# Last phase of a decoder block: attention rows and their norms moved into the first MLP, head norms in token blocks, transposes released earlier

## The chip, the cores and the metric

The kernel runs on one core of one Trainium2 chip. A core has TensorE (PE in the profile, its weight loads PEld), VectorE (DVE), ScalarE (ACT), GpSimd (POOL), and SyncE (SP), which here only issues DMAs. The metric is the device time of one execution, in microseconds: 1348.08 is the median of three runs (1347.18 to 1348.21).

## The reference

Eight sequences of 512 tokens with 256 features pass through a layer norm and causal attention (16 heads), then cross attention to a short context followed by an MLP, then a second MLP with ternary weights. In short:

```
x1  = x  + attention(layernorm(x)) @ Wout + bout
Q   = layernorm(x1)                           # the residual base of the cross block
q   = layernorm(Q)*g1+b1 @ wq                 # 16 heads of 64
qn  = q / max(||q||_head, 1e-12)
x'  = Q + (qn . N) + bo                       # N = keys, values and wo folded per sequence
x2  = x1 + x' + gelu(layernorm(x')*g2+b2 @ w1 + b1) @ w2 + b2
out = x2 + gelu(layernorm(x2) @ W1t + b1) @ W2t + b2
```

Since cross attention has no softmax, the context side is folded into one matrix N per sequence before this phase.

## The kernel before

The program has four phases, one after the other: projections, attention, preparation of N and the ternary weights, and `mix_phase` (L1392 to L2126), in which everything after attention is computed. Only the last one is changed, besides a table of constants (`head_selectors`, L82). It fills the trace from about 625 us to the end.

All weights and features are in two parts, a rounded high part and a low part (`fh`/`fl`, `bh`/`bl`, `hh`/`hl`), and a product is three matmuls. A round of `mix_phase` works on two sequences at once: the front of one (attention rows, query tiles, cross attention) and the back of the one before it (both MLPs). There are nine rounds: one with a front only, seven with both (six of them load more work, the seventh loads none), and one with a back only. Below they are rounds 0 to 8.

A round is a list of units in a fixed order: `order(back, front)` (L1417) gives 8 query tiles Q, 8 tiles M of the first MLP, 8 cross tiles X, and 8 tiles T of the ternary MLP. PE *begins* a unit (`begin`, which fills one of three PSUM tiles `psG`) and *finishes* it three units later (`finish`, `rows_of`: 12 matmuls of 256 columns that add to row sums in `psY`). In between, ACT and DVE (for X also POOL) make the high and low parts of the unit. Each engine's program is written out by hand in that same order, and each works through its own queue in order. T is a stage of its own: Q, M and X run on into one another, T starts and ends with an empty pipeline.

`psY` is two pairs of banks. Pair 0 holds the rows of M, then of X; pair 1 holds the norms' head sums, then the attention rows, then the rows of T. A pair must be read by DVE before PE opens it again (`pair_free`, `open_rows` L1966).

Normalised rows `z` are transposed by PE into the single PSUM tile `psT`, one half of the features at a time: `z_first` waits for `z`, `z_second` waits until the low part of the first half is made (`z_parts`), `z_split` does so for the second half. This happens three times a round:

- z1, the query norm of the *next* sequence: attention rows on PE after the last M unit, `add_attention` on DVE in X unit 5, `moments` in X unit 7, `rsqrt_twice` on POOL, `z1` in T unit 2, transposes after T units 4 and 6 (`Z1_AT`). In round 0 `z1` and its transposes stand after X, so that round 1 begins behind them.
- z2, for M: made by DVE at the head of a round, transposed after Q units 3 and 5 (`Z2_AT`). In round 8 it stands alone before M.
- z3, for T: from `add_mlp` and its moments on DVE in X unit 2, transposed after X units 4 and 6.

The head norms of q: ACT squares the query tiles, `head_sums` adds them over heads on PE into a 128x512 tile (32 rows for each of four query tiles, all 512 tokens), ACT takes the root after M unit 3 (`NORMS_AT`), DVE inverts and splits (`inverse_norms`, L1773 to L1780), all over 512 columns:

```
stepped(nc.vector.tensor_scalar(n2[:, :], n2[:, :], 1e-12, None, ALU.max))
stepped(nc.vector.reciprocal(n2[:, :], n2[:, :]))
stepped(nc.vector.tensor_copy(rh[:, :], n2[:, :]))
```

POOL adds biases at the head of a round (`biased`, three operations over 128x1024), and adds `base` later, once DVE has read the old one (`base_free`). DVE's `prepare_o` makes the high and low parts of the next attention output, also at the head of a round.

## Time and profile before

| | us |
|---|---|
| median of three runs | 1348.08 |
| the profiled execution | 1350.23 |
| its span, first to last instruction | 1348.4 |
| PE busy over the span | 1046.7 (78%) |
| DVE / ACT / POOL busy | 788.7 / 663.5 / 425.9 |
| one middle round, query tile to query tile | 79.86 |
| PE busy in it | 72.04 |

The page gives busy time for the whole program, and the last phase is about half of it. For this change the timeline of PE in one round is the view to read: whatever stops PE there is listed behind its rows in brackets, as the idle time before the instruction and the line it waited at (L1966 opens a pair, L1986 `z_first`, L1991 `z_second`, L1996 `z_split`, L2023, L2035 and L2045 wait for the parts of an M, X and T unit, L2060 for the inverse norms). The median stands 2.15 us below the profiled execution.

### The profile page before, as it was taken

What the parts mean: (1) busy time and instruction counts of PE and PEld (TensorE: products, weight loads), DVE (VectorE), ACT (ScalarE), POOL (GpSimd) and SP (SyncE); (2) the same over time, 40 slices, a digit from 0 to 9 for tenths busy, and PEclk for the clock granted to TensorE, in tenths of its full rate; (3) what the DMA queues carried; (4) which work ended last, traced back from release to release, by engine and by line L of the source; (5) the groups of instructions that cost most, each with busy time, mean ns of one, the idle gap of its engine ahead of it and who ended that gap; (6) DMA issues with size and microseconds to landing.
All of it is one profiled execution on the core that took longest, in us unless ns stands there. A gap on an engine that the chain in (4) does not pass through costs nothing. (4 is left out here: it accounts for less than half of the span.)

```text
span 1348.4 us, 22433 instructions
## 1 busy us (share of the span) xinstructions
PE 1046.7 (78%) x6749; PEld 751.9 (56%) x6749; DVE 788.7 (58%) x1680; ACT 663.5 (49%) x1166; POOL 425.9 (32%) x556
## 2 busy tenths in 40 slices
PE   3777058788999985783566989899898999988875
PEld 2444023343444433672454877778687786867764
DVE  3888356576777743863444655746656574655523
ACT  1334115565666673461225466473655747465433
POOL 0344226566333331110422231524313242330301
PEclk9677558999999996896777999999999999999987
DMA  2332423333222103257202040301203030020000
GB/s 85 103 116 74 124 92 111 114 120 105 90 96 93 58 31 135 117 223 287 57 26 84 1 125 0 109 16 44 81 0 116 8 108 16 0 78 1 10 7 16
DMA packets 52716, 103.72 MB, mean 77 GB/s; under 512 B 6640, under 2 KB 32496, under 8 KB 48560
## 3 DMA queue, kind: packets, MB, share of 16 engines
q1 hardware_dynamic: 49484, 95.53, 21.0%
q0 software_dynamic: 1920, 6.03, 1.4%
q10 hardware_dynamic: 1252, 1.39, 0.3%
q8 instruction: 33, 0.54, 0.2%
q14 instruction: 27, 0.22, 0.1%
HBM read 62.96 MB, written 39.58 MB: 76 GB/s over the span
## 5 line engine op out<-in xcount | busy, mean ns | idle before, releaser
L804 ACT ACTIVATE p_probs<-p_psS 128x512 f32<-128x512 f32 (+1 forms) x352 | 180.8, 563 | 122.3 <-ACTq L803 120.0
L706 DVE CUSTOM_DVE_ANT_0 p_psA<-p_psA,p_mask 128x512 f32<-128x512 f32 (+1 forms) x256 | 155.5, 647 | 103.9 <-DVEq L704 103.6
L1771 DVE TENSOR_TENSOR p_hl<-p_h,p_hh 128x512 fp32r<-128x512 f32 x128 | 86.9, 688 | 153.1 <-DVEq L1770 151.1
L838 PE MATMUL p_psA<-p_ks,p_qs 96*128 96x512 bf16 (+3 forms) x512 | 144.1, 317 | 37.0 <-PEq L836 36.7
L857 PE MATMUL p_psS<-p_qs,p_ks 99*128 99x256 bf16 (+3 forms) x512 | 131.1, 310 | 20.0 <-PEq L882 11.4
L1656 ACT ACTIVATE p_h<-p_psG,w_columns 128x512 f32<-128x512 f32 x128 | 88.3, 690 | 94.4 <-ACTq L1655 94.0
L725 POOL TENSOR_SCALAR_AFFINE_SELECT p_probs<-p_probs 128x512 f32<-128x512 f32 x128 | 80.8, 635 | 130.8 <-POOLq L724 113.8
L1975 PE MATMUL p_psY<-p_n,p_hh 128*128 128x256 f32 x512 | 105.3, 289 | 12.5 <-PEq L2035 7.6
L868 PE MATMUL p_psO<-p_probs,p_v 128*32 128x512 f32 (+3 forms) x1024 | 92.8, 457 | 26.6 <-PEq L864 25.2
L857 PEld LDWEIGHTS p_psS<-p_qs,p_ks 99*128 99x128 bf16 x512 | 44.0, 98 | 106.8 <-issue 91.8
L1697 ACT ACTIVATE p_hh<-p_h 128x512 fp32r<-128x512 f32 x64 | 40.4, 632 | 118.8 <-ACTq L1696 118.8
L1975 PEld LDWEIGHTS p_psY<-p_n,p_hh 128*128 128x128 f32 x512 | 84.4, 192 | 18.9 <-issue 18.1
L1616 POOL TENSOR_TENSOR p_base<-p_x,p_q0b 128x1024 f32<-128x1024 f32 x8 | 19.2, 2405 | 223.2 <-POOLq L1615 223.2
L1657 ACT ACTIVATE p_hh<-p_psG,w_columns 128x512 fp32r<-128x512 f32 x128 | 87.8, 686 | 0.0
L838 PEld LDWEIGHTS p_psA<-p_ks,p_qs 96*128 96x128 bf16 x512 | 51.6, 101 | 59.5 <-issue 47.4
L1975 PE MATMUL p_psY<-w_w_hi,p_hh 128*128 128x256 f32 x256 | 72.4, 283 | 11.1 <-PEq L2023 11.1
L1981 PE MATMUL p_psT<-p_ident,p_z 128*128 128x128 f32 x192 | 32.7, 298 | 57.8 <-PEq L1986 31.6
L1975 PE MATMUL p_psY<-p_n,p_hl 128*128 128x256 f32 x256 | 72.8, 284 | 0.0
L1975 PE MATMUL p_psY<-w_t,p_hh 128*128 128x256 f32 x256 | 65.3, 291 | 8.8 <-PEq L1966 4.7
L1975 PE MATMUL p_psY<-w_w_hi,p_hl 128*128 128x256 f32 x256 | 71.5, 279 | 0.0
L1975 PE MATMUL p_psY<-w_w_lo,p_hh 128*128 128x256 f32 x256 | 71.3, 279 | 0.0
L710 DVE TENSOR_REDUCE p_mx<-p_psA 128x2 f32<-128x512 f32 (+1 forms) x96 | 66.3, 693 | 3.8 <-DVEq L704 0.6
(244 smaller groups left out, 2811.6 us busy)
## 6 DMA issues: line engine op xcount, KB each, us to landing
p_n<-n_parts SPq DMA_DIRECT2D x16, 1024.0 KB, 6.8
o_sums<-p_o SPq DMA_DIRECT2D x32, 256.0 KB, 2.9
n_parts<-p_nh SPq DMA_DIRECT2D x8, 1024.0 KB, 3.9
n_parts<-p_nl SPq DMA_DIRECT2D x8, 1024.0 KB, 6.0
q_parts<-p_part SPq DMA_DIRECT2D x48, 128.0 KB
p_qs<-q_parts SPq DMA_DIRECT2D x32, 192.0 KB
p_x<-in_x_dram SPq DMA_DIRECT2D x8, 512.0 KB, 4.2
p_qs<-q_parts SPq DMA_DIRECT2D x32, 128.0 KB
```

The lines of the kernel that those rows point to most:

```text
L706: nc.vector.tensor_tensor_reduce(out=bank[:, 0:w], in0=bank[:, 0:w], in1=mask[:, S - w:S], scale=1.0, scalar=MASKED, op0=ALU.add, op1=ALU.max,
L710: nc.vector.tensor_reduce(mx[:, h:h + n, i], bank[:, 0:n * w].rearrange("p (r k) -> p r k", r=n), AX_X, ALU.max).then_inc(A_free, 1)
L725: nc.gpsimd.affine_select(square, square, [[0, G], [1, P]], ALU.is_ge, 0.0, base=0, channel_multiplier=-1).then_inc(masked, 1)
L804: nc.scalar.activation(probs[:, g % 2, at:at + n * w], psS[place(s, turn) % SB][:, 0:n * w], ACT.Exp, scale=SCALE).then_inc(exp_done, 1)
L838: last = nc.tensor.matmul(bank[:, z * w:(z + 1) * w], qs[0:SROWS, k, g * G + r0 + z, i * P:(i + 1) * P], ks[0:SROWS, k, g, 0:w], start=Tru ...
L857: last = nc.tensor.matmul(bank[:, z * w:(z + 1) * w], key, qs[0:SROWS + MROWS, k, h, j * P:S], start=True, stop=True)
L868: last = nc.tensor.matmul(psO[32 * r:32 * r + 32, j * P:S], v[:, k, g, j, :], probs[:, g % 2, at:at + w], start=(j == 0), stop=(j == TT - 1))
L1656: nc.scalar.activation(h[:, u % LAG, :], psG[u % LAG][:, :], ACT.Gelu, bias=bias[:, m:m + 1])
L1657: nc.scalar.activation(hh[:, u % LAG, :], psG[u % LAG][:, :], ACT.Gelu, bias=bias[:, m:m + 1]).then_inc(h_ready, 1)
L1697: nc.scalar.activation(hh[:, s, :], h[:, s, :], ACT.Copy).then_inc(qh_dve if m < POOL_FROM else qh_pool, 1)
L1771: nc.vector.tensor_tensor(hl[:, s, :], h[:, s, :], hh[:, s, :].bitcast(F32), ALU.subtract).then_inc(h_parts, 1)
L1975: last = nc.tensor.matmul(dst, xx[:, toks], ww[:, k, :], start=(k == 0 and t % 2 == 0 and i == 0), stop=(last_k and t % 2 == 1 and i == le ...
```

## The change

Four things are done.

1. **Attention rows and z1 move forward.** In rounds with a back, PE's attention rows come after M unit 2 (`ROWS_AT`) instead of after M unit 7; DVE's `add_attention`, `moments` and `z1` come at M units 3, 4 and 6; POOL's `rsqrt_twice` stands before z3's; the transposes of z1 come after M unit 6 and X unit 0, and ACT reads them after X units 0 and 2. In round 0 the attention rows stand before X and z1 within X. In round 7, z2 of the last round is made and transposed within T.
2. **Norms by token blocks.** The four groups of 32 rows now hold the four blocks of 128 tokens, and all 16 heads (high and low copy) within each. The root, the maximum, the reciprocal and the rounding work on 128x128; four small operations write the low/high signs into a block-diagonal `rs` (128x512, cleared once). `head_sums` is 16 matmuls of 128 columns instead of 4 of 512. ACT takes the root after M unit 1.
3. **`psT` is free once read.** A new semaphore `T_free` is raised by ACT behind a drain after it has read the tile twice (`affine`), or by DVE after `plain_low`; `z_first` and `z_second` wait for it, and `z_split` for both low parts.
4. **`base`** is made in `q0b` at the head of the round, without waiting for the old one.

```diff
-        Z1_AT = (4, 6)
-        NORMS_AT = 3
+        Z1_AT, Z1_READ = (M, 6, X, 0), (0, 2)
+        Z1_FIRST, Z1_FIRST_READ = (3, 5), (5, 7)
+        NORMS_AT, ROWS_AT, ADD_AT, MOMENTS_AT, Z1_MADE = 1, 2, 3, 4, 6
...
-        n2 = sb("n2", [P, S], F32)
-        rh, rs = sb("rh", [P, S], F32R), sb("rs", [P, S], F32R)
+        n2 = sb("n2", [P, P], F32)
+        rh, rs = sb("rh", [P, P], F32R), sb("rs", [P, S], F32R)
...
                     biased(q0b, q0, B2).then_inc(pool_step, 1)
+                    pool.wait_ge(pool_step, 1)
+                    pool.sem_inc(pool_step, -1)
+                    nc.gpsimd.tensor_tensor(q0b[:, :, :], x1[:, :, :], q0b[:, :, :], ALU.add).then_inc(base_ready, 1)
                     if more:
                         rows_in()
-                    pool.wait_ge(pool_step, 1)
-                    pool.sem_inc(pool_step, -1)
-                    if back:
-                        pool.wait_ge(base_free, 1)
-                        pool.sem_inc(base_free, -1)
-                    nc.gpsimd.tensor_tensor(base[:, :, :], x1[:, :, :], q0b[:, :, :], ALU.add).then_inc(base_ready, 1)
+                if more:
+                    rsqrt_twice()
...
                 nc.scalar.activation(hi[:, c, :], psT[:, :], ACT.Identity, bias=b[:, c:c + 1], scale=g[:, c:c + 1]).then_inc(z_done, 1)
+                act.drain().then_inc(T_free, 1)
...
                         nc.scalar.activation(hh[:, s, :], h[:, s, :], ACT.Copy).then_inc(qh_dve if m < POOL_FROM else qh_pool, 1)
+                        read = Z1_READ if back else Z1_FIRST_READ
+                        if more and m in read:
+                            affine(fh, w["ln1_g"], w["ln1_b"], read.index(m))
...
-                nc.vector.scalar_tensor_tensor(out=rs[:, :], in0=rh[:, :].bitcast(F32), scalar=minus, in1=n2[:, :],
-                                               op0=ALU.mult, op1=ALU.add).then_inc(rn_ready, 1)
+                for b in range(TB):
+                    rows = slice(32 * b, 32 * b + 32)
+                    last = nc.vector.scalar_tensor_tensor(out=rs[rows, b * P:(b + 1) * P], in0=rh[rows, :].bitcast(F32),
+                                                          scalar=minus[rows, :], in1=n2[rows, :], op0=ALU.mult, op1=ALU.add)
+                last.then_inc(rn_ready, 1)
...
                         if not back and m == XT - 1:
                             inverse_norms()
+                            add_attention(False)
+                            stepped(moments(x1))
+                            aggregate(mv1, var1_ready)
...
             def z_second():
-                pe.wait_ge(z_parts, 1)
-                pe.sem_inc(z_parts, -1)
+                pe.wait_ge(T_free, 1)
+                pe.sem_inc(T_free, -1)
                 transpose_rows(1)
...
-                for r in range(4):
-                    last = nc.tensor.matmul(sums[32 * r:32 * r + 32, :], select[:, j, :], sq[:, (4 * j + r) % SQ, :],
-                                            start=(j == 0), stop=(j == 1))
+                for t in range(4 * j, 4 * j + 4):
+                    for b in range(TB):
+                        last = nc.tensor.matmul(sums[32 * b:32 * b + 32, 0:P], select[:, t, :], sq[:, t % SQ, b * P:(b + 1) * P],
+                                                start=(t == 0), stop=(t == XT - 1))
...
-                            if kind == M and m == XT - 1 and front and more:
+                            if more and back and kind == M and m == ROWS_AT:
                                 attention_rows()
...
+                            if more and back and (kind, m) == Z1_AT[:2]:
+                                z_first()
+                            if more and back and (kind, m) == Z1_AT[2:]:
+                                z_second()
```

What the change does to the order shows on DVE first. In the names, `p_hl` is the low part of a unit, `p_n` the norms, `p_x<-p_psY,p_xin` is `add_attention`, `p_x<-p_psY,p_base` is `add_mlp`, `p_h<-p_psG,p_q` scales a cross tile. This is DVE in a middle round, from the end of `prepare_o` through the M units, before:

```order
L1733 TENSOR_TENSOR p_ol<-p_o,p_oh 128x1024
L1771 TENSOR_TENSOR p_hl<-p_h,p_hh 128x512 x5
L1776 TENSOR_SCALAR p_n<-p_n 128x512
L1777 RECIPROCAL p_n<-p_n 128x512
L1778 CAST p_rh<-p_n 128x512
L1779 SCALAR_TENSOR_TENSOR p_rs<-p_rh,p_select,p_n 128x512
L1771 TENSOR_TENSOR p_hl<-p_h,p_hh 128x512 x3
```

and after:

```order
L1734 TENSOR_TENSOR p_ol<-p_o,p_oh 128x1024
L1773 TENSOR_TENSOR p_hl<-p_h,p_hh 128x512 x2
L1778 ISA
L1779 TENSOR_SCALAR p_n<-p_n 128x128
L1780 RECIPROCAL p_n<-p_n 128x128
L1781 CAST p_rh<-p_n 128x128
L1784 SCALAR_TENSOR_TENSOR p_rs<-p_rh,p_signs,p_n 32x128 x4
L1773 TENSOR_TENSOR p_hl<-p_h,p_hh 128x512 x2
L1739 TENSOR_TENSOR p_x<-p_psY,p_xin 128x512 x2
L1823 ISA
L1824 ISA
```

The inverse norms have moved from behind the fifth low part to behind the second, and `add_attention` now stands behind the fourth, in front of the fifth to eighth.

Next, still DVE in a middle round, the end of M and the start of X (`p_stats<-p_x` are moments, of `x2` when they follow `add_mlp`), before:

```order
L1785 TENSOR_TENSOR p_h<-p_psG,p_q 128x512 x2
L1790 TENSOR_TENSOR p_hl<-p_h,p_hh 128x512 x2
L1738 TENSOR_TENSOR p_x<-p_psY,p_base 128x512 x2
L1799 ISA
L1875 ISA
L1744 BN_STATS p_stats<-p_x 128x6 x4
L1785 TENSOR_TENSOR p_h<-p_psG,p_q 128x512
L1749 BN_AGGR p_mv<-p_stats 128x2 x4
L1790 TENSOR_TENSOR p_hl<-p_h,p_hh 128x512
```

and after:

```order
L1745 BN_STATS p_stats<-p_x 128x6 x4
L1750 BN_AGGR p_mv<-p_stats 128x2 x4
L1773 TENSOR_TENSOR p_hl<-p_h,p_hh 128x512 x2
L1755 TENSOR_SCALAR p_z<-p_x,p_mv,p_both 128x256 x4
L1773 TENSOR_TENSOR p_hl<-p_h,p_hh 128x512
L1791 TENSOR_TENSOR p_h<-p_psG,p_q 128x512 x2
L1796 TENSOR_TENSOR p_hl<-p_h,p_hh 128x512 x2
L1739 TENSOR_TENSOR p_x<-p_psY,p_base 128x512 x2
L1805 ISA
L1745 BN_STATS p_stats<-p_x 128x6 x4
L1791 TENSOR_TENSOR p_h<-p_psG,p_q 128x512
L1750 BN_AGGR p_mv<-p_stats 128x2 x4
```

The moments of the attention rows and `z1` now stand between the low parts of M units 4 to 7, so the last low part and the first scaled cross tile come behind `z1`.

Last, ACT in a middle round from the last M unit through X (`p_hh<-p_h` is the high part of a cross tile, `p_bh<-p_psT` a read of z3), before:

```order
L1656 ACTIVATE p_h<-p_psG,w_columns 128x512
L1657 ACTIVATE p_hh<-p_psG,w_columns 128x512
L1697 ACTIVATE p_hh<-p_h 128x512 x7
L1673 ACTIVATE p_bh<-p_psT 128x512
L1697 ACTIVATE p_hh<-p_h 128x512
L1673 ACTIVATE p_bh<-p_psT 128x512
```

and after:

```order
L1659 ACTIVATE p_hh<-p_psG,w_columns 128x512
L1697 ACTIVATE p_hh<-p_h 128x512
L1669 ACTIVATE p_feat<-p_psT,w_columns 128x512
L1670 ACTIVATE p_fh<-p_psT,w_columns 128x512
L1697 ACTIVATE p_hh<-p_h 128x512 x2
L1669 ACTIVATE p_feat<-p_psT,w_columns 128x512
L1670 ACTIVATE p_fh<-p_psT,w_columns 128x512
L1697 ACTIVATE p_hh<-p_h 128x512 x4
L1676 ACTIVATE p_bh<-p_psT 128x512
```

The two pairs of reads of z1 stand now behind the first and the third cross tile; before they stood among the T units.

## Rows read from the trace of the kernel before

**Rows 1.** Busy time by stretch: length, then busy us (instructions) per engine, clock, DMA.
```profile
660.93:721.50 60.57, 37.23 (x200) 30.19 (x201) 30.21 (x51) 18.46 (x30) 22.16 (x18) 0.78 0.18 61
...
801.75:881.61 79.86, 72.04 (x458) 60.79 (x457) 47.74 (x90) 45.70 (x71) 25.48 (x21) 1.00 0.16 53
...
1201.01:1287.55 86.54, 70.05 (x434) 58.60 (x433) 43.56 (x79) 43.52 (x69) 19.32 (x13) 0.97 0.04 13
```

**Rows 2.** Timeline, PE, one middle round: start us, us, line, instruction, idle before it.
```profile
812.43 0.63 PE L1981 MATMUL p_psT<-p_ident,p_z 128*128 128x128 f32 x4 [1.64 <-PEq L1991]
...
822.29 0.33 PE L1975 MATMUL p_psY<-w_w_hi,p_hh 128*128 128x256 f32 x1
...
838.08 0.35 PE L1975 MATMUL p_psY<-w_w_hi,p_hh 128*128 128x256 f32 x1 [1.58 <-PEq L2023]
...
842.86 0.28 PE L1975 MATMUL p_psY<-w_wout_hi,p_oh 128*128 128x256 f32 x1
...
852.07 0.36 PE L1975 MATMUL p_psY<-p_n,p_hh 128*128 128x256 f32 x1 [1.00 <-PEq L2035]
...
861.41 0.47 PE L1960 MATMUL p_psG<-p_bh,w_t 128*128 128x512 f32 x1 [0.28 <-PEq L1996]
...
880.59 0.36 PE L1975 MATMUL p_psY<-w_t,p_hh 128*128 128x256 f32 x1 [0.51 <-PEq L2045]
```

**Rows 3.** Timeline, PE, the last round that has a query stage.
```profile
1244.78 0.35 PE L1975 MATMUL p_psY<-p_n,p_hh 128*128 128x256 f32 x1 [2.32 <-PEq L1966]
...
1260.45 0.47 PE L1960 MATMUL p_psG<-p_bh,w_t 128*128 128x512 f32 x1 [0.15 <-PEq L1996]
...
1276.26 0.36 PE L1975 MATMUL p_psY<-w_t,p_hh 128*128 128x256 f32 x1 [0.51 <-PEq L2045]
```

**Rows 4.** Timeline, PE, the first round, and the two joins at either end.
```profile
685.27 1.62 PE L2063 MATMUL p_psG<-p_rs,w_spread_sel 128*128 128x512 f32 x3 [7.97 <-PEq L2060]
...
689.12 0.55 PE L1975 MATMUL p_psY<-p_n,p_hh 128*128 128x256 f32 x1 [2.23 <-PEq L1966]
...
714.21 1.08 PE L1981 MATMUL p_psT<-p_ident,p_z 128*128 128x128 f32 x4 [6.16 <-PEq L1986]
...
721.50 0.76 PE L1960 MATMUL p_psG<-p_fh,w_wq_hi 128*128 128x512 f32 x1 [2.56 <-PEq L1996]
...
742.43 0.33 PE L1975 MATMUL p_psY<-w_w_hi,p_hh 128*128 128x256 f32 x1
...
1280.72 0.63 PE L1981 MATMUL p_psT<-p_ident,p_z 128*128 128x128 f32 x4 [3.29 <-PEq L1986]
...
1287.55 0.77 PE L1960 MATMUL p_psG<-p_bh,w_w_hi 128*128 128x512 f32 x1 [2.56 <-PEq L1996]
```

**Rows 5.** Lines by form, L868 in the attention phase: count, busy us, mean ns.
```profile
L868 PE MATMUL p_psO<-p_probs,p_v 128*32 128x512 f32 x184 | 24.6, 602 | 11.4 <-PEq L864 11.4
...
L868 PE MATMUL p_psO<-p_probs,p_v 128*32 128x128 f32 x176 | 8.9, 273 | 0.0
```

**Rows 6.** Timeline, DVE: the first round's end, and the same middle round.
```profile
708.20 1.29 DVE L1738 TENSOR_TENSOR p_q<-p_psY,p_q 128x512 f32<-128x512 f32 x2 [2.52 <-DVEq L1823]
...
810.26 2.02 DVE L1761 TENSOR_TENSOR p_bl<-p_feat,p_bh 128x512 fp32r<-128x512 f32 x1 [3.65 <-DVEq L1760]
...
815.39 1.22 DVE L1731 TENSOR_TENSOR p_o<-p_o,p_ol 128x1024 f32<-128x1024 f32 x1
...
832.51 3.35 DVE L1777 RECIPROCAL p_n<-p_n 128x512 f32<-128x512 f32 x1
```

**Rows 7.** Timeline, POOL, the same middle round.
```profile
811.70 2.83 POOL L1589 TENSOR_TENSOR p_xin<-p_xin,p_biases 128x1024 f32<-128x1024 f32 x1
...
861.48 0.20 POOL L1566 TENSOR_TENSOR p_var<-p_mv,p_eps 128x4 f32<-128x4 f32 x1
...
865.85 0.20 POOL L1586 TENSOR_TENSOR p_both<-p_var,p_rstd 128x4 f32<-128x4 f32 x1 [0.18 <-POOLq L1568]
```

**Rows 8.** Timeline, ACT, just before the same middle round.
```profile
796.61 0.78 ACT L1667 ACTIVATE p_feat<-p_psT,w_columns 128x512 f32<-128x512 f32 x1 [0.47 <-ACTq L1666]
```

More of the change, by code:

```diff
@@ L1676, in round_ @@
                 units = order(back, front)
-                if back and not front:
-                    for c in range(C):
-                        affine(bh, w["ln2_g"], w["ln2_b"], c)
                 for u, (kind, m) in enumerate(units):
@@ L1704, in round_ @@
                         gelu(w["fb1"], u, m)
-                        if more and m in Z1_AT:
-                            affine(fh, w["ln1_g"], w["ln1_b"], Z1_AT.index(m))
-                if more and not back:
-                    for c in range(C):
-                        affine(fh, w["ln1_g"], w["ln1_b"], c)
+                        if front and not more and m == XT - 1:
+                            for c in range(C):
+                                affine(fh, w["ln2_g"], w["ln2_b"], c)
             act.wait_ge(act_go, 1)
@@ L1925, in round_ @@
                             aggregate(mv2, var2_ready)
-                        if more and m == 5:
-                            affine_low(fl, fh, 0)
-                        if more and m == 7:
-                            affine_low(fl, fh, 1)
+                        if front and not more and m == 5:
+                            z2()
+                        if front and not more and m == 7:
+                            for c in range(C):
+                                affine_low(fl, fh, c)
             nc.vector.memset(eps[:, :], EPS)
+            nc.vector.memset(rs[:, :].bitcast(F32), 0.0)
             stepped(nc.vector.memset(mhalf[:, :], -0.5))
@@ L2070, in round_ @@
                 stages = [units[:-XT], units[-XT:]]
-                if back and not front:
-                    z_first()
-                    z_second()
-                    z_split()
                 at = 0
@@ L2105, in round_ @@
                                 z_second()
-                            if kind == T and more and m == Z1_AT[0]:
+                            if front and not more and kind == T and m == 7:
                                 z_first()
-                            if kind == T and more and m == Z1_AT[1]:
-                                z_second()
                     at += len(stage)
-                if more and not back:
-                    z_first()
-                    z_second()
+                if not back:
+                    z_split()
             for i in range(2):
                 pe.sem_inc(pair_free[i], 1)
+            pe.sem_inc(T_free, 1)
             pe.wait_ge(consts, 1)
```

129 lines of the change are left out of this document (73 added, 56 removed).

## The prediction

> **What bounds the kernel now.** I read the busy time by stretch first, then PE's timeline of one middle round, and then, wherever PE stands idle in it, the other engines at that moment.
>
> A middle round takes 79.86 us, of which PE is busy 72.04 at a clock of 1.00 [rows 1]. DVE has 47.7, ACT 45.7 and POOL 25.5. So PE is the bound of these rounds, and what can be won is the idle time between its instructions. The first stretch of the phase is different: of 60.57 us PE is busy 37.23, at a mean clock of 0.78. The reader is to see that the ends of the phase are far looser than its middle.
>
> In a middle round PE is idle at [rows 2]: the second transposes of z2 (1.64, it waits for a low part), the last M units (1.58, DVE is in the inverse norms), an X unit (1.00), the start of T (0.28) and its last units (0.51). The rest lies in T, where z1 is transposed. At the ends: 7.97 for the inverse norms of round 0; transposes at 714.21 and query tiles at 721.50 behind X in round 0; and 3.29 and 2.56 before M of round 8 [rows 4].
>
> **Middle rounds, 1 to 6.** I cut the round at four places where PE's timeline has a row before, and build the same stretch for after. Units from the same timeline: a tile of six matmuls 1.41 us, 12 rows matmuls 1.40, 24 of them (attention rows) 2.80, a spread of X 0.24, four transposes 0.36 plus 0.2 when PE had been idle. These are spacings of the rows around those in [rows 2].
>
> *Query to the first M rows* (801.75 to 822.29, 20.54 us). `z_second` no longer waits for DVE, only for ACT's two reads: PE is there at 810.6, ACT is done at about 810.3. That gives back 1.64 and the restart, 2.0. Two things are lost. POOL now runs four operations of 2.4 us in a row at the head of the round, not three. DVE's low part at 810.26 shows what this means: 2.02 us where it needs 0.69, because it starts only when POOL's operation ends at 811.70; and the POOL operation that begins there takes 2.83, longer by DVE's part [rows 6, 7]. They alternate. So the second low part is done at about 815.2 and M begins 0.4 late; `prepare_o`, which starts at 815.39 now, starts at 817.5 and ends at 820.9; M's first low part comes behind it at 821.5, where PE asks at 820.6: 1.0 lost. Sum: 20.54 - 2.0 + 0.4 + 1.0, less 0.1 for restarts: 19.85.
> The Trainium skill has this twice. Advanced Engine Details and Errata, section "Mode Summary", says that GpSimd and DVE block each other when DVE is in a two-port mode; by that alone a low part, a sum of two tensors, would not be held, and the round would keep the 1.4 us. GPSIMD Engine Reference, section "Key points", adds DVE operations with two inputs in SBUF. The row at 810.26 is such an operation and was held, so the sum goes by it.
>
> *M rows to the end of M* (822.29 to 842.86, 20.57 us). The wait of 1.58 goes. The reciprocal takes 3.35 us over 512 columns [rows 6], so about 0.85 over 128; the whole of `inverse_norms` falls from 5.4 to about 2.4, and comes where PE does not ask for it. Added: attention rows 2.8 and the first transposes of z1, 0.55. The path of z1 just fits: attention rows end at 831.5, add 1.5, a low part 0.6, moments 1.4 and their aggregation 0.5, POOL's chain 4.6 (861.48 to 866.05, [rows 7]), z1 1.4, together 10.2; PE has 7 x 1.41 + 0.24 = 10.1 of units in between. Sum: 20.57 - 1.8 + 2.8 + 0.55 = 22.1.
>
> *X* (842.86 to 861.41, 18.55 us with 2.8 of attention rows in it). Those rows stood on PE while DVE added the MLP's sums, which X's rows wait for (they share a pair of banks). Without them the wait is open. Round 7 loads no attention rows and shows the price: 2.32 us at 1244.78 [rows 3]. The change adds to it. ACT now reads z1 between the first and the second cross tile, two operations of 0.67 (the row at 796.61 has 0.78 with its tail, [rows 8]) and a drain, and DVE's `add_mlp` stands behind the low part of that second tile: 1.7 more, so 4.0. The second transposes cost 0.5, and the two low parts of z1 on DVE, 0.6 each, come before the third and fourth unit of the chain DVE, ACT, POOL, so the wait of 1.00 at 852.07 grows to 1.6. Sum: 18.55 - 2.8 + 4.0 + 0.5 + 0.6, less 0.6 of small idle behind that wait: 20.2.
>
> *T* (861.41 to 881.61, 20.20 us). z1 leaves it. Round 7's T has no z1: from its start to its last wait it takes 1276.26 - 1260.45 = 15.81, a middle round 880.59 - 861.41 = 19.18 [rows 2, 3]. That is 3.37 less: 16.85.
>
> The round comes to 19.85 + 22.1 + 20.2 + 16.85 = 79.0, a gain of 0.9 of a round. The four stretches change by -0.7, +1.5, +1.7 and -3.4. Round 1 counts from its first M rows, so five and three quarters of these: -5.
>
> **Head sums.** They become 64 records of 128 columns in place of 16 of 512 in each round. Kept concurrent over the four column groups, the columns are the same and the cost is 0. The attention phase has both shapes: 184 records of 512 in 24.6 us and 176 of 128 in 8.9 [rows 5], 0.134 and 0.051 each. By these 32 records take 1.6 us where 8 take 1.07, the most it can cost: 0.55 for each group, 16 groups, 9 us. I take 0, as the 8.9 us hold the tail behind each group, and keep 9 as a bound.
>
> **Round 0 and its join to round 1.** Before X, 7.97 of idle [rows 4] shrinks by the shorter inverse norms (3.0) and root (0.35), but attention rows (2.8) fill that time and DVE adds them (3.4 with moments) before it scales the first cross tile. X's rows start at 688.3 instead of 689.12: -0.8. Attention rows leave X: -2.8. X ends at 704.5, where it now ends about 708.0 (DVE's next operation is at 708.20, [rows 6]). From there PE now has to wait for moments, z1, and twice for transposes, ACT and DVE, until 721.50 [rows 4]: 13.5 us. All of this lies within X after the change, and the queries of round 1 begin at 704.6: -16.9. Two covers go with it. z2 still needs X's result: add 1.5, `base` 1.3, moments and aggregation 1.9, POOL 1.5, z2 1.4, so it is ready at 712.3, and PE asks at 710.2: 2.1. And POOL's four operations start 4.3 us later against PE than in a middle round, so M's first low part comes 3.2 late, 2.2 more than above. Against these stands the slow start of the query tiles (0.76 at 721.50, 1.5 in all). Sum at the first M rows of round 1 (now 742.43): -16.9 + 2.1 + 2.2 - 1.5 = about -14.
>
> **Round 7, round 8.** Round 7 gains 1.6 in Q (no `prepare_o` behind the low parts) and 1.6 in M: -3.2. z2 of round 8 is made within T of round 7. PE is done there at 1277.4 and begins M at 1287.55 [rows 3, 4]. After, the second transposes wait for ACT's reads of the first (0.9 and 0.55 of their own), the last rows end at 1278.45, ACT reads until 1278.95, DVE's low part ends at 1279.65, M begins at 1279.8: -7.7. And M begins at the high clock: the first tile at 1287.55 shows 0.77 for a matmul that takes 0.47 at 861.41 [rows 2, 4], about 1.9 over four microseconds. Sum -12.8.
>
> The prologue has one wait shortened by DVE's low part (0.7) and two copies of constants more or larger on SP's queue. I take 0, with a microsecond either way.
>
> **Sum.** -5 -14 -12.8 = -31.8: the profiled execution of 1350.2 becomes 1318.4, its span 1316.6. The median of the runs is 2.15 below the profiled one, so the runs come to 1316.3.
>
> **The rivals.**
> *A, the clock falls in X.* PE idles 4.0 us before X's rows in each middle round. In the trace it idled 3.29 us before 1280.72 and ran the next transposes at 2.4 GHz (0.63 for four), but 6.16 us before 714.21 and ran at 1.2 GHz (1.08) [rows 4]. Four microseconds lie between. If it falls, the rows from 689.12 (0.55 each at the start) show what follows: about 2.5 us lost before the clock is back, some hidden by the wait of 1.6. Also here: `T_free` comes as late as the low part did, 1.8 a round. Either gives 1316.3 + 6 x 2 = 1328.
> The Trainium skill (TensorE: Matmul & The Clock Gate, section "Part 1: The HAM clock gate") says that the slow state is the default and that idleness brings it back, which speaks for this rival; the trace agrees at 714.21, and not yet at 1280.72.
> *B, the middle rounds gain more.* POOL's fourth operation does not hold up `prepare_o`, and ACT's reads slip in behind the second tile: then 1.4 and 1.7 a round go. 1316.3 - 6 x 2.5 = 1301. For it: DVE in a middle round is busy 47.7 of 79.86. Against: both engines work in order, and the order is written.
> *C, slower.* The place is the start of X in the middle rounds. There z1's chain, the last low part of M, two scaled tiles, their low parts, `add_mlp`, moments and the third tile all stand in one queue on DVE, and POOL's chain of seven small operations in front of it can hold DVE up, as at 810.26. If each wait in it is longer by as much as the one there (1.3 us) at four places and the clock falls (2.5), a round costs 7.7 more than I say: 1316.3 + 46 = 1362. It decides from 5.3 a round, where it eats 31.8. For it: PE has no spare work there after the change. Against: DVE's operations that read PSUM show no such stretch while POOL works.
> *D, the head sums cost their upper bound*: 1316.3 + 9 = 1325. And the change does not do what it says if z1 is not ready at M unit 6 and PE stands there: this is inside C.
>
> **How the numbers follow.** My forecast (the middle rounds between -2.3 and +1 each) 0.58, A 0.15, D 0.04, B 0.15, C 0.08. The forecast's own range is 1308 to 1326. With A, D and half of B it is 1303 to 1334. Differences of under 0.2% (2.7 us) cannot be told from none. Only C is slower, with 0.07 of its 0.08; 0.02 lie within 0.2%; faster 0.91.
>
> **What would show it.** In the profile after: a middle round near 79.0; PE idle 3.5 to 4.5 us before the first cross rows and a clock of 1.00 behind it; idle about 1 us before the first M rows; `z_second` of z2 without a wait; T's 8 units in 16.8; a reciprocal of 0.9; query tiles of round 1 directly behind X of round 0; and M of round 8 some 2.4 us behind T of round 7. Wrong it would be with a middle round over 84, or with the clock below 0.95 in one.

## The result and the profile after

The changed kernel takes 1339.67 us (median of seven runs, 1334.74 to 1341.04) where the kernel before takes 1348.65 on the same chip. The ratio is 0.9908 (95% interval 0.9886 to 0.9929): 9 us are gained where 32 were forecast, and the time lies outside the range. The profiled execution took 1340.68, its span 1338.7.

The page of the changed kernel, its span and clock line:

```profile
span 1338.7 us, 23286 instructions
...
PEclk9677558899999996897689899898999989999997
```

The reader is to see the 8s and 7s in the second half of the clock line, one dip in each round. Before, that part was nines. The same in the windows view (stretch; us; busy us of PE, PEld, DVE, ACT, POOL; then PE's clock): round 2 in its four stretches, then all of it, then from the query tiles of round 7 to M of round 8. They answer to [rows 1].

```profile
793.82:813.66 19.84, 19.14 (x141) 14.45 (x139) 13.53 (x17) 16.83 (x27) 10.25 (x4) 1.00 0.08 26
813.66:836.64 22.98, 22.46 (x157) 20.88 (x157) 12.93 (x31) 10.59 (x17) 3.28 (x7) 1.00 0.25 68
836.64:858.80 22.16, 17.54 (x117) 16.46 (x115) 13.37 (x27) 7.93 (x13) 9.54 (x8) 0.85 0.00 0
858.80:875.69 16.89, 15.74 (x96) 13.59 (x97) 9.40 (x20) 9.90 (x16) 1.84 (x3) 1.00 0.32 124
793.82:875.69 81.87, 74.88 (x506) 65.37 (x505) 49.23 (x93) 45.25 (x71) 24.91 (x21) 0.96 0.15 51
1203.10:1279.49 76.39, 69.46 (x482) 59.86 (x481) 42.15 (x81) 43.16 (x69) 18.85 (x13) 1.00 0.02 8
```

A middle round takes 81.87 us, 2.0 more than before, with the clock at 0.85 in its third stretch. PE's timeline, first the join of rounds 0 and 1, then the waits of round 2, then rounds 7 and 8; the rows before are [rows 2 to 4]:

```profile
641.64 0.55 PE L1995 MATMUL p_psY<-w_wout_hi,p_oh 128*128 128x256 f32 x1 [23.14 <-PEq L1986]
...
662.43 0.76 PE L1980 MATMUL p_psG<-p_fh,w_wq_hi 128*128 128x512 f32 x1 [2.56 <-PEq L2018]
...
690.38 0.55 PE L1995 MATMUL p_psY<-p_n,p_hh 128*128 128x256 f32 x1 [5.21 <-PEq L1986]
...
707.33 0.39 PE L1980 MATMUL p_psG<-p_fh,w_wq_hi 128*128 128x512 f32 x1
...
715.62 0.63 PE L2001 MATMUL p_psT<-p_ident,p_z 128*128 128x128 f32 x4 [2.46 <-PEq L2008]
...
725.50 0.47 PE L1980 MATMUL p_psG<-p_bh,w_w_hi 128*128 128x512 f32 x1 [0.48 <-PEq L2018]
...
731.82 0.35 PE L1995 MATMUL p_psY<-w_w_hi,p_hh 128*128 128x256 f32 x1 [0.69 <-PEq L1986]
...
813.66 0.36 PE L1995 MATMUL p_psY<-w_w_hi,p_hh 128*128 128x256 f32 x1 [0.67 <-PEq L1986]
...
834.51 0.63 PE L2001 MATMUL p_psT<-p_ident,p_z 128*128 128x128 f32 x4 [0.52 <-PEq L2008]
...
840.68 0.55 PE L1995 MATMUL p_psY<-p_n,p_hh 128*128 128x256 f32 x1 [3.65 <-PEq L1986]
...
843.38 1.05 PE L2001 MATMUL p_psT<-p_ident,p_z 128*128 128x128 f32 x4
...
851.43 0.36 PE L1995 MATMUL p_psY<-p_n,p_hh 128*128 128x256 f32 x1 [0.81 <-PEq L2058]
...
858.80 0.48 PE L1980 MATMUL p_psG<-p_bh,w_t 128*128 128x512 f32 x1 [0.17 <-PEq L2018]
...
1243.97 0.36 PE L1995 MATMUL p_psY<-p_n,p_hh 128*128 128x256 f32 x1 [2.65 <-PEq L1986]
...
1279.49 0.47 PE L1980 MATMUL p_psG<-p_fh,w_w_hi 128*128 128x512 f32 x1 [1.60 <-PEq L2018]
```

Query tiles of round 1 begin at 707.33 directly behind X, and M of round 8 follows the last rows of T after 1.60 idle; both ends work as they were meant to. In round 2 PE waits 3.65 before X's rows (840.68) and the first matmul there takes 0.55, where the one of round 7, after a wait of 2.65 (1243.97), takes 0.36: the clock is at 1.2 GHz in the one and at 2.4 in the other. Slow rows run until 846.

Cut where the forecast cut, in the profiled executions:

| stretch | forecast | measured |
|---|---|---|
| start of the last phase to the queries of round 0 | 0 | +1.5 |
| those to the first M rows of round 1 | -14 | -12.1 |
| those to the queries of round 7 | -5 | +12.7 |
| those to M of round 8 | -10.9 | -10.2 |
| M of round 8 to the end | -1.9 | -1.6 |
| sum | -31.8 | -9.7 |

The +1.5 is not the change's: the last burst of matmuls of the phase ahead of it begins 1.7 later in this trace (615.40 against 613.67). This start moves from kernel to kernel: in the profiles of this case the queries of round 0 begin anywhere from 656.8 to 665.1. Of the 22 us that are missing, 17.7 lie in the middle rounds. Those are what the experiments are about.

### The profile page after: what moved, and what is told of

Read it like the earlier page. It is cut to its first block and busy times, and to the rows that moved or that the text cites. A ratio compares the mean times of both kernels' runs of the same rounds, so it can differ in the third digit from the quotient of the medians.

```text
span 1338.7 us, 23286 instructions
## 1 busy us (share of the span) xinstructions
PE 1062.5 (79%) x7133; PEld 781.2 (58%) x7133; DVE 798.1 (60%) x1705; ACT 660.4 (49%) x1166; POOL 423.2 (32%) x556
## 5 line engine op out<-in xcount | busy, mean ns | idle before, releaser
L1995 PE MATMUL p_psY<-p_n,p_hh 128*128 128x256 f32 x512 | 117.2, 313 | 35.8 <-PEq L1986 29.7
L1995 PEld LDWEIGHTS p_psY<-p_n,p_hh 128*128 128x128 f32 x512 | 95.6, 218 | 41.8 <-issue 41.3
L1571 POOL TENSOR_TENSOR p_var<-p_mv,p_eps 128x4 f32<-128x4 f32 x24 | 8.1, 338 | 334.0 <-POOLq L1577 201.8
L1995 PE MATMUL p_psY<-p_n,p_hl 128*128 128x256 f32 x256 | 78.9, 308 | 0.0
L1604 POOL TENSOR_TENSOR p_hl<-p_h,p_hh 128x512 fp32r<-128x512 f32 x40 | 51.3, 1295 | 46.0 <-POOLq L1603 35.1
```

Of the source, the lines that this page charges most:

```text
L1604: nc.gpsimd.tensor_tensor(hl[:, s, :], h[:, s, :], hh[:, s, :].bitcast(F32), ALU.subtract).then_inc(qn_pool, 1)
L1995: last = nc.tensor.matmul(dst, xx[:, toks], ww[:, k, :], start=(k == 0 and t % 2 == 0 and i == 0), stop=(last_k and t % 2 == 1 and i == le ...
```

## The experiments

Times are compared as ratios to the kernel before, run beside each on the same chip (1349 to 1354 us there). "A round" is the distance from the first query tile of one middle round to that of the next in the kernel's profile; rounds 2 to 6 of a kernel agree within 0.1 us, but for the run with 4 idle matmuls and that with only short norms (79.20 in round 2, 79.0 in the others).

| run | ratio (95%) | a round |
|---|---|---|
| before | 1 | 79.86 |
| the change | 0.9908 (0.9886-0.9929) | 81.87 |
| 14 idle matmuls before X's rows | 0.9791 (0.9769-0.9813) | 79.93 |
| 4 idle matmuls there | 0.9852 (0.9816-0.9888) | 81.64 |
| reads of z1 one unit later | 0.9799 (0.9772-0.9825) | 79.72 |
| that, and z1's transposes after M 7 | 0.9826 (0.9792-0.9860) | 79.63 |
| pairs of banks exchanged | 0.9874 (0.9849-0.9899) | 81.87 |
| that, and another order on DVE | 0.9769 (0.9727-0.9811) | 79.29 |
| attention rows late again | 0.9724 (0.9702-0.9747) | 77.74 |
| only short norms, on before | 0.9907 (0.9877-0.9938) | 78.99 |
| only the early release, on before | 0.9872 (0.9844-0.9900) | 77.63 |
| rows late, POOL's base in M | 0.9692 (0.9663-0.9720) | 77.15 |
| that, and z1's turn in T | 0.9666 (0.9635-0.9697) | 76.32 |
| that, with POOL's base in X | 0.9627 (0.9591-0.9663) | 75.52 |

**Is it the clock?** Work for PE that nobody reads, put into the wait:

```diff
+    if more and back:            # rounds 1 to 6, first cross rows
+        open_rows(T_PAIR)
+        for i in range(14):
+            nc.tensor.matmul(psY[2 * T_PAIR][:, :], w["spread_sel"][:, i % XT, :], rs[:, :], start=True, stop=True)
     open_rows(X_PAIR)
```

> The changed kernel, with 14 idle matmuls of 128x512 put on PE directly before the first cross rows of rounds 1 to 6 (into the pair of banks that stands free there; nothing reads them). They fill 3.3 of the 3.65 us in which PE waits there and take nothing away. Clock theory: the clock stays at 1.00 through X, where it now runs at half speed for 5.7 us; the first cross rows take 1.44 a unit instead of 2.7. That is 2.7 us a round, of which the chain of DVE, ACT and POOL may keep 0.7: a round falls from 81.87 to about 79.8, the time from 1340 to about 1328. Rival, the chain sets the pace of X: the clock is 1.00 but the later waits of X grow by what the rows save, the round loses under 0.5 us and the time stays above 1337. Third, the idle matmuls end late or the clock falls all the same: 1340 or more.

Measured: 0.9791 and 79.93 us a round. The windows row of a middle round, then PE's rows at that place:

```profile
875.21:955.14 79.93, 75.73 (x521) 65.41 (x520) 48.37 (x93) 45.18 (x71) 25.18 (x21) 1.00 0.16 52
```

```profile
918.77 1.18 PE L2066 MATMUL p_psY<-p_rs,w_spread_sel 128*128 128x512 f32 x4 [0.43 <-PEq L1987]
...
922.11 0.28 PE L1996 MATMUL p_psY<-p_n,p_hh 128*128 128x256 f32 x1
...
929.18 0.35 PE L1996 MATMUL p_psY<-p_n,p_hh 128*128 128x256 f32 x1 [1.30 <-PEq L2059]
```

The clock is 1.00 and the first cross row takes 0.28. X's rows begin as late as ever (27.05 us behind the first M rows, 27.0 in the changed kernel), so nothing but the clock differs, and it is worth 1.94 us a round. The wait at a later unit grew from 0.81 to 1.30, which is the part that the chain keeps. The clock theory is shown.

**Shorter wait instead of idle work.** ACT's reads of z1 go behind cross tiles 1 and 3:

```diff
-        Z1_AT, Z1_READ = (M, 6, X, 0), (0, 2)
+        Z1_AT, Z1_READ = (M, 6, X, 0), (1, 3)
```

> The changed kernel, with ACT's two reads of the transposed z1 put behind cross units 1 and 3 instead of 0 and 2 (low parts and the wait for both moved by one unit). The low part of the second cross tile on DVE then doesn't wait 1.5 us for ACT, and PE's wait before the cross rows falls from 3.65 to about 2.4, as in round 7 (2.65, clock held). Clock theory: a round gains 1.2 by the wait and 2 more by the clock, 78.7 instead of 81.87, the time is about 1321. Rival, the chain: only part of the 1.2 is kept, as the second transposes come later, 1334 or more.

Measured: 0.9799, 79.72 a round, wait 2.29. The gain is real but 1 us a round smaller than the clock theory said. Two middle rounds of this kernel:

```profile
867.59:947.31 79.72, 73.84 (x506) 64.18 (x505) 49.14 (x93) 45.15 (x71) 24.98 (x21) 0.98 0.16 53
1027.11:1106.82 79.71, 72.49 (x507) 62.70 (x505) 49.00 (x93) 45.16 (x71) 24.94 (x21) 1.00 0.16 53
```

The clock fell in the first (it was slow for 3.4 us of X) and held in the second, and both last the same. It fell in four of the six middle rounds. Of rounds 2 to 6 the three with the fall take 79.71 to 79.80, the two without it 79.71 and 79.74. So here a short fall costs under 0.1 us, and the missing microsecond isn't the clock's: even with the clock held X takes 17.43 us from its first rows to T, where the run with 14 idle matmuls takes 16.16. That the chain DVE, ACT, POOL sets the pace there is my reading; no run takes it apart. The rival was half right: the earlier rows are given back, but the time is well below its 1334.

**How long must the wait be?** As the first run, with 4 idle matmuls:

```diff
-        for i in range(14):
+        for i in range(4):
```

> The run with 14 idle matmuls before the cross rows, with 4 of them instead. They take 0.95 us and leave PE idle for 2.7 where the changed kernel has 3.65. Theory: the clock falls for the length of the idle time; 2.65 in round 7 and 2.29 in the run with later reads kept it, so 2.7 keeps it: 79.9 a round as with 14, 2.1% below the kernel before. Rival: the clock is held only by work that fills the whole wait: 81.9 and 0.9%.

Measured: 0.9852; rounds 3 to 6 take 81.64, 81.43, 81.10 and 79.97. Their windows, then PE's first cross rows in rounds 3, 6 and 7:

```profile
876.47:958.11 81.64, 75.26 (x511) 65.03 (x509) 49.13 (x93) 45.24 (x71) 24.91 (x21) 0.98 0.15 51
958.11:1039.54 81.43, 75.22 (x511) 64.95 (x510) 49.08 (x93) 45.24 (x71) 24.93 (x21) 0.98 0.15 52
1039.54:1120.64 81.10, 75.06 (x510) 64.96 (x509) 49.18 (x93) 45.23 (x71) 24.91 (x21) 0.98 0.16 52
1120.64:1200.61 79.97, 73.71 (x511) 63.55 (x509) 48.37 (x93) 45.13 (x71) 25.16 (x21) 1.00 0.09 33
```

```profile
923.35 0.36 PE L1996 MATMUL p_psY<-p_n,p_hh 128*128 128x256 f32 x1 [2.06 <-PEq L1987]
...
1167.51 0.35 PE L1996 MATMUL p_psY<-p_n,p_hh 128*128 128x256 f32 x1 [2.06 <-PEq L1987]
...
1241.48 0.55 PE L1996 MATMUL p_psY<-p_n,p_hh 128*128 128x256 f32 x1 [2.65 <-PEq L1987]
```

The wait is 2.06 in each of these rounds (0.42 more lies ahead of the idle matmuls). In rounds 1 to 5 the clock fell within 1.5 us of the first row, in round 6 it held. In round 7 a wait of 2.65 dropped it before the first row, where the same wait kept it in the changed kernel. My theory that the length of one wait decides is refuted. Its premise was misread too: the 2.29 of the run with later reads, which it takes as kept, lost the clock in four rounds of six. Over all profiled executions, the wait before the first cross rows and how often the clock fell, before them or within 1.5 us behind:

| wait, us | where | clock fell |
|---|---|---|
| 1.83 | later reads and z1 after M 7, rounds 1 to 6 | 2 of 6 |
| 2.06 | 4 idle matmuls, rounds 1 to 6 | 5 of 6 |
| 2.29 | later reads, rounds 1 to 6 | 4 of 6 |
| 2.28 to 2.32 | round 7 of six kernels, before among them (held) | 4 of 6 |
| 2.65 | round 7 of six kernels, the change among them (held) | 3 of 6 |
| 3.65 | the change, rounds 1 to 6 | 6 of 6 |

So between 1.8 and 2.7 us it can go either way.
The Trainium skill (TensorE: Matmul & The Clock Gate, section "Part 1: The HAM clock gate") says that what the monitor watches is free-running, is not reset when a kernel starts, and that the point of a change of clock varies with it. That fits what equal waits did here, once one way and once the other; no run here shows that it is the cause.

The slow stretch is only 3.4 us in these rounds, half as long as the 6.8 of the changed kernel, and yet costs up to 1.7. DVE's rows show how, in round 2 and in round 6 (in each the second low part of z1, then two of the four parts of z3):

```profile
846.99 0.69 DVE L1763 TENSOR_TENSOR p_fl<-p_feat,p_fh 128x512 fp32r<-128x512 f32 x1 [0.65 <-DVEq L1762]
...
847.60 1.70 DVE L1756 TENSOR_SCALAR p_z<-p_x,p_mv,p_rstd 128x256 f32<-128x256 f32 x2
...
1172.09 0.68 DVE L1763 TENSOR_TENSOR p_fl<-p_feat,p_fh 128x512 fp32r<-128x512 f32 x1
...
1172.69 0.73 DVE L1756 TENSOR_SCALAR p_z<-p_x,p_mv,p_rstd 128x256 f32<-128x256 f32 x2
```

Measured from the first cross row (841.62 and 1167.51), the low part of z1 comes at 5.4 in round 2 and at 4.6 in round 6. z1's second transposes stand behind the slow rows, ACT reads them late, DVE waits 0.65 for ACT, and the parts of z3 then take 1.70 in place of 0.73, since POOL's low part begins beside them (847.86). In the run with reads one unit later DVE asks for them later, and there the fall is free. So the fall is dear where z1's second half stands right behind the slow rows, as in the changed kernel, whose parts of z3 take 1.71 there (846.76).

**Is it the pair of banks?**

```diff
-        M_PAIR, A_PAIR, X_PAIR, T_PAIR = 0, 1, 0, 1
+        M_PAIR, A_PAIR, X_PAIR, T_PAIR, N_PAIR = 0, 1, 1, 0, 1
```

> The changed kernel, with two pairs of banks exchanged: cross rows go into the pair that the attention rows leave free after M unit 3, ternary rows into the pair of the MLP's rows. PE then doesn't wait for DVE's sum of the MLP before the first cross rows (3.65 us idle). Theory: the wait before X rows goes (they start at 837 instead of 840.7 on the scale of round 2), but DVE scales the third cross tile only behind that sum and its moments, so PE stands about 3.5 us before the rows of the third tile. It begins those rows 3 us earlier than now. If the clock holds, a round is near 78.5 and the time 1320; if it falls at the new wait, near 80.5 and 1332. Rival, the chain that carries X starts at the DVE sum and not at the pair of banks: the time stays within 4 us of 1340.

Measured: 0.9874, 81.87 a round. PE's two new waits in round 2:

```profile
848.48 0.36 PE L1995 MATMUL p_psY<-p_n,p_hh 128*128 128x256 f32 x1 [2.81 <-PEq L2055]
...
852.05 0.55 PE L1995 MATMUL p_psY<-p_n,p_hh 128*128 128x256 f32 x1 [1.01 <-PEq L2058]
```

The wait before X's rows is down to 0.42, and two others stand for it at the third and fourth tile, with 2.81 and 1.01. The clock falls a microsecond behind the first of them, at 849.50, and stays low for 6.8 us. The round is as long as with the change, as the rival had it, and longer than both of my numbers; the ratio is lower by 0.3%, with intervals that touch. So the pair of banks alone isn't what holds X. The clock fell in this run too, so by itself it doesn't part the queue on DVE from the clock.

Next, the queue in another order: DVE scales the third tile before the MLP's sum and the fourth before its moments, z3 is made in one piece, and POOL's root stands behind its first low part. The expectation puts the fall of the clock behind the second wait; by the windows it was behind the first.

```diff
                         if back and m == 2:
                             scaled_low((u - 2) % LAG)
                             scaled_low((u - 1) % LAG)
-                            add_mlp(old)
-                            moments(x2).then_inc(step, 1)
                         scaled(s, m)
+                        if back and m == 2: add_mlp(old)
...
+                        if back and m == 3: stepped(moments(x2)); aggregate(mv3, var3_ready)
...
                         if back and m == 4:
-                            norm3((2, 3), True)
+                            norm3(range(TT), True)
```

> The changed kernel with the pairs of banks exchanged as in the run before, ACT's reads of z1 behind cross units 1 and 3, and another order on DVE and POOL in X: DVE scales the third tile before it sums the MLP and the fourth before the moments, z3 is made in one piece behind the fifth; POOL makes the low part of the fourth tile before the root for z3. The run with exchanged pairs alone had two waits, 2.81 at the third unit and 1.01 at the fourth, and the clock fell behind the second. Theory: without the queue on DVE both waits shrink below 1 us, the clock holds; X takes about 15.5 instead of 18.1 us after its first rows, and these come 3.5 earlier: a round of 76 to 77 instead of 81.9, 2.6 to 2.8% below the kernel before. Rival: the rows of X are set by the chain DVE, ACT, POOL (three engines for each tile) and the wait comes back at a later tile: a round of 79 to 80, 1.8 to 2.1% below.

Measured: 0.9769, 79.29 a round. Three waits of 1.00, 1.01 and 1.59 stand in X at a clock of 1.00. At each PE waits for the parts of a cross tile (L2057). The round is the rival's (79 to 80). Its cause, a chain over three engines, fits these waits but wasn't tested apart.

**Does the first part of the change pay at all?** Attention rows back between M and X and z1 in T in the middle rounds, the rest kept:

```diff
-        NORMS_AT, ROWS_AT, ADD_AT, MOMENTS_AT, Z1_MADE = 1, 2, 3, 4, 6
+        NORMS_AT, ROWS_AT = 1, 7
+        Z1_LATE = (4, 6)
...
+                        if back and more and m == 5:
+                            add_attention(False)
```

> The changed kernel with the first of its four parts undone in rounds 1 to 6: attention rows stand between the last M unit and X, and z1 is made and transposed within T, as before. Kept are the short norms, the early release of the transposes, the base in q0b and both ends of the phase (rounds 0, 7 and 8). Clock theory: attention rows cover the sum on DVE, the clock stays at 1.00, and a round is 79.86 less 1.6 (wait at the last M units) less 2.0 (second transposes of z2) plus 1.4 (POOL's fourth operation at the head) = about 77.7; against 81.87 that is 25 us: 1315. Rival: the move forward costs little, the ends and the norms give all there is: 1330 or more.

Measured: 0.9724 and 77.74 us a round, as forecast. So moving attention rows and z1 forward costs 4.1 us in each middle round, 1.9 by the clock and 2.2 otherwise, where the other parts bring 2.1. Over the whole kernel it takes two thirds of their gain.

**What the other parts bring alone.** On the kernel before, the second and the third part of the change, each by itself, as the diff ahead of the prediction has them:

```diff
-        NORMS_AT = 3
+        NORMS_AT = 1
-        n2 = sb("n2", [P, S], F32)
+        n2 = sb("n2", [P, P], F32)
```
```diff
             def z_second():
-                pe.wait_ge(z_parts, 1)
+                pe.wait_ge(T_free, 1)
```

> The kernel before, with only the norms by token blocks (128x128 for root, maximum, reciprocal and rounding; the root after M unit 1). Theory: the wait of 1.58 us at the last M units goes in seven rounds, and 3.3 us in round 0: 14 us or 1.0% below the kernel before, head sums at the same 1.07 us. Rival, the head sums in four times as many matmuls, or four small sign operations on DVE, eat it: under 0.5% below.

> The kernel before, with only the early release of the transposes (second transposes wait for ACT's reads and not for DVE's low part). Theory: the wait of 1.64 us and a restart, together 2.0, go in Q of seven rounds, plus about 0.5 in T where z1 is transposed: 17 us or 1.3% below. Rival: M's start waits for the second low part instead, which POOL's work holds up: under half of that, 0.6% or less.

Measured: short norms 0.9907 and 0.87 us a round, the time as forecast and the round half of it, since a wait of 0.37 stays among the M units. Head sums take 1.08 for 32 records. Early release 0.9872 and 2.23 a round, near the forecast of 2.0 and 0.5: 1.54 lie ahead of the first M rows and 0.69 in T. Both together would give 76.8; the run with late rows has 77.74. The rest, about 0.9, lies ahead of the first M rows (19.87 us with late rows, 19.00 with the early release alone), and is what POOL's fourth operation at the head of the round takes. In the changed kernel DVE's first step of `prepare_o` shows it, beside the same step alone at the start of the phase; POOL's operation of the moment stands under them:

```profile
637.59 1.23 DVE L1732 TENSOR_TENSOR p_o<-p_o,p_ol 128x1024 f32<-128x1024 f32 x1 [10.03 <-DVEq L1731]
...
807.12 3.43 DVE L1732 TENSOR_TENSOR p_o<-p_o,p_ol 128x1024 f32<-128x1024 f32 x1
```

```profile
806.61 2.85 POOL L1594 TENSOR_TENSOR p_xin<-p_xin,p_biases 128x1024 f32<-128x1024 f32 x1
```

It takes 3.43 in place of 1.23, since it begins only when POOL's has ended. It is a product of two tensors in SBUF. The Trainium skill (GPSIMD Engine Reference, section "Key points") counts such operations among those that contend with GpSimd: by that rule, the trace agrees.

**Better versions.** First that operation is held back until DVE is in M (a semaphore that DVE raises behind M unit 2). Then z1's second transposes go behind T unit 7. Then the operation is released by the MLP's sum in X, as in the kernel before.

```diff
+                    if more and back:       # POOL
+                        rows_in()
+                        pool.wait_ge(base_go, 1)
                     nc.gpsimd.tensor_tensor(q0b[:, :, :], x1[:, :, :], q0b[:, :, :], ALU.add).then_inc(base_ready, 1)
...
+                        if more and m == NORMS_AT + 1:      # DVE, M; third run: behind add_mlp in X
+                            nc.vector.engine_nop().then_inc(base_go, 1)
...
-        Z1_LATE = (4, 6)
+        Z1_LATE = (4, 7)                    # second and third run
```

> The run with late attention rows (77.74 us a round), with POOL's fourth operation at the head of the round (the sum for the base) held back until DVE is behind M unit 2, where POOL is idle. Theory, POOL holds DVE up: prepare_o and the second low part of z2 end earlier, M's first rows come 1.2 to 1.4 us earlier, a round is 76.4, 3.3 to 3.5% below the kernel before. Rival: the low parts of the M units then take longer and PE waits there, or the hold-up was not POOL's: 77.5 to 78, 2.8% as it was.

> The run with POOL's fourth operation held back (77.15 us a round), and z1's second transposes put behind T unit 7 instead of 6, ACT's reads of them behind its last T unit. In that run PE waits 1.13 us before them and 0.96 before the last rows of T. Theory: both waits go, the low part of z1 comes about 0.5 late for the next query tiles: 76.0 us a round, 3.7% below the kernel before. Rival: the whole wait comes back before the query tiles: 77 and 3.1%.

> As the run beside it (second transposes behind T unit 7), but POOL's sum for the base is released by DVE's sum of the MLP in X, as in the kernel before, and not in M. Theory, from adding stretches of the runs with one part each: M and X together keep 0.2 us less (38.2 in place of 38.6), a round of 75.7. Rival: POOL is late for z3's root behind that operation of 2.4 us and T starts later: 76.5 or more.

Measured: 0.9692, 0.9666, 0.9627; rounds of 77.15, 76.32 and 75.52. In the first the head of the round gains 0.9, but M loses 0.3 of it. In the second the wait before the last rows of T goes (0.96) and the other stays (1.15): 0.83 gained for 1.15 expected. The expectation has the place of the other wrong. It stands before z1's *first* transposes, which begin as soon as DVE has made z1, and so a later place of the second ones can't touch it:

```profile
930.61 0.63 PE L2012 MATMUL p_psT<-p_ident,p_z 128*128 128x128 f32 x4 [1.15 <-PEq L2019]
```

```profile
928.93 1.38 DVE L1764 TENSOR_SCALAR p_z<-p_x,p_mv,p_both 128x256 f32<-128x256 f32 x4
```

The third run is the fastest kernel here, 3.7% below before and 2.8% below the change (its interval touches that of the run ahead of it, the rounds are 0.8 apart). Its gain lies in X: 15.49 from the first cross row to T, 15.5 to 15.6 in the kernel before, and 16.34 in the run ahead of it. With late rows and the operation still at the head of the round X takes 16.34 as well. So making `base` early costs X 0.85 us on top of the 0.9 at the head. M keeps its loss with the operation in X (22.2 from its first rows to X's, 22.0 with late rows), so that loss isn't the operation's. The two last parts of z3 on DVE show part of it. First DVE and POOL with the operation in M, then with it in X:

```profile
910.16 2.49 DVE L1764 TENSOR_SCALAR p_z<-p_x,p_mv,p_rstd 128x256 f32<-128x256 f32 x2
```

```profile
909.93 2.56 POOL L1606 TENSOR_TENSOR p_hl<-p_h,p_hh 128x512 fp32r<-128x512 f32 x2 [1.26 <-POOLq L1605]
```

```profile
912.20 1.09 DVE L1764 TENSOR_SCALAR p_z<-p_x,p_mv,p_rstd 128x256 f32<-128x256 f32 x2
```

```profile
911.46 1.36 POOL L1606 TENSOR_TENSOR p_hl<-p_h,p_hh 128x512 fp32r<-128x512 f32 x1 [0.66 <-POOLq L1605]
...
913.22 1.30 POOL L1606 TENSOR_TENSOR p_hl<-p_h,p_hh 128x512 fp32r<-128x512 f32 x1 [0.40 <-POOLq L1605]
```

The same two operations take 2.49 beside a pair of POOL's low parts that run back to back, and 1.09 where these stand apart. The Trainium skill (Advanced Engine Details and Errata, section "Mode Summary") says that GpSimd and two-port instructions of DVE block each other. The trace agrees as far as DVE's two operations end when POOL's pair does (912.65 and 912.49); whether they ran in a two-port mode no row shows. The price here is 1.4 us, from the rows.

**The wait in M.**

```diff
-        Z1_AT, Z1_READ = (M, 6, X, 0), (1, 3)
+        Z1_AT, Z1_READ = (M, 7, X, 0), (1, 3)
```

> The run in which ACT reads z1 behind cross units 1 and 3 (79.7 us a round), with z1's first transposes behind M unit 7 instead of 6. There PE waits 0.53 us for them, of the 0.9 by which the stretch of M came out longer than forecast. Theory: that wait and the restart behind it go, nothing else moves: 79.1 a round, 0.3 to 0.4% less time than that run (2.3% below the kernel before). Rival: the time comes back in front of the cross rows, since those wait for DVE's sum in any case: 79.6 to 79.8, 2.0% below.

Measured: 0.9826, 79.63 a round against 79.72. The 0.53 goes and comes back: PE waits 0.74 at an M unit and 1.35 at the third cross tile, while the wait before the first shrinks to 1.83. The rival holds; the ratios of the two runs do not differ by more than their intervals.

## Why the prediction was wrong, point by point

- **Step that failed: the start of X in the middle rounds.** The forecast had PE idle for 4.0 us there with the clock held. The wait came nearly as forecast, 3.65 at 840.68, and the clock fell, in each of the six rounds. This is rival A, which had a chance of 0.15 and a price of 2.0 a round; measured, 1.94. The chance rested on a row read too short: behind the 3.29 us of idle at 1280.72 the clock held only for the four transposes. Windows of the kernel before show that it fell within a microsecond of their start (the granted clock is the 1.00 and the 0.50):

```profile
1280.72:1281.60 0.88, 0.63 (x4) 0.39 (x4) 0.00 (x0) 0.13 (x1) 0.00 (x0) 1.00 1.00 343
1281.65:1283.90 2.25, 0.00 (x0) 0.03 (x1) 0.69 (x1) 1.27 (x2) 0.00 (x0) 0.50 0.01 2
```

So both waits that I weighed, 3.29 and 6.16, had lost the clock, and 0.15 was on the wrong side of them. The experiments show that waits of 1.8 to 2.8 are already in doubt. X took 22.16 us in place of 20.2.
- **M, mis-sized.** 22.98 in place of 22.1. z1's chain took 10.3 us, from the end of the attention rows (823.9) to z1 ready (834.2); I had 10.2 against 10.1 of units and called it just fitting (the terms as written add to 10.0). The wait for z1 is 0.52, at 834.51; no run takes apart the other 0.36 of the 0.88. That is 5 us over the rounds. A later place doesn't bring it back (79.63 against 79.72 a round).
- **Query to the first M rows:** 19.84 for 19.85, and that is luck: the early release gives 1.54 there where I took 2.0, and POOL's fourth operation costs 0.9 where I took 1.4. Two errors of 0.5 cancel. **T:** 16.89 for 16.85.
- **Round 0 and the join:** -12.1 for -14. X's first rows came 27.95 behind the queries (28.2 before), 0.6 short of the step; X and the queries of round 1 each gave 0.6 to 0.8 less than their terms. z2 waited 2.46 for 2.1.
- **Rounds 7 and 8:** -11.8 for -12.8, with 1.60 before M of round 8 (1279.49). Its first matmul takes 0.47, at the high clock, as forecast.
- **Head sums:** 1.08 for 32 records, where 8 took 1.07: 0, as taken. Rival D falls.
- **Prologue:** 0 as taken, once the late start of the phase is counted.
- **Rivals B and C.** B (a round gains more) did not come. C, which made the whole slower, did not come either, but its place was right: most of the missing time went at the start of X in the middle rounds.

With rival A and the M term the forecast's own sum gives 1328 + 5 = 1333; the join (1.9), rounds 7 and 8 (1.0), and the later start of the phase (1.7) bring it to 1338, and the measured median is 1339.67.

## What to carry to other kernels

Work that looks movable may be the cover of a wait: the attention rows hid a sum on DVE, and their move opened 3.65 us on the bounding engine, which cost the clock as well. So ask what each moved step now hides, and treat an opened wait of about 2 us or more on TensorE as a likely loss of the clock (3 in 6 to 6 in 6 of the cases here), priced by what stands right behind it. Read the clock for some microseconds behind a wait, and not only at the first instruction. And add the parts of a change one by one: here all of the change but one move gained 2.8%, and that move in the middle rounds took 1.8% back. Another part, the early `base`, cost 0.9 us a round at its head and 0.85 in X.

## What the runs showed of the hardware

- Equal waits of PE do not always end alike: 2.65 us kept the clock in three kernels and lost it in three; 2.06 lost it in five rounds and kept it in the sixth, in one execution. Even 1.83 lost it in two rounds of six.
- The fall can come behind the wait: after 2.81 us idle in the kernel with exchanged banks the clock fell 1.0 us behind the first row, after 3.29 in the kernel before 0.9 us behind it, when four transposes had run at 2.4 GHz [rows 4].
- A slow stretch of 3.4 us can cost nothing, or 1.7 us, by which instructions stand in it: with the clock as a mean over the round (0.98 in both) the two cannot be told apart.
- Two `tensor_scalar` operations of DVE took 0.73, 1.09, 1.70 or 2.49 us by where POOL's work stood against them.

Left open: why equal waits end differently, where the rest of M's excess lies, and how much of the 0.8 us by which the last version is faster comes from those two operations alone.
